# One kernel for a scan block and two MLPs: fewer jobs in the preparation stage, in a deeper pipeline, and other engines for two of its operations

## Time and profile before

| | |
|---|---|
| median of 3 runs | 3308.22 us |
| the profiled execution | 3307.34 us |
| its span (first to last instruction) | 3305.5 us |
| busy: TensorE / VectorE / ScalarE / POOL | 3123.4 / 2032.1 / 998.7 / 1085.0 us |
| granted TensorE clock, mean | 0.983 |
| matmuls of the MLP stage (L809, L825) | 750.9 + 743.6 us |
| matmuls of the gated MLP (L682, L703) | 539.3 + 523.8 + 523.3 us |

### The profile page before, as it was taken

The page is one execution under the profiler, slowest core; times in us unless marked ns, Lnnn a source line. Parts: engine busy times, 40 slices in busy tenths (PEclk is TensorE's granted clock), DMA queues, the critical chain, the costliest instruction groups (busy, mean ns, idle before and its releaser), DMA issues.

```text
span 3305.5 us, 43287 instructions
## 1 busy us (share of the span) xinstructions
PE 3123.4 (94%) x15308; PEld 2523.5 (76%) x15308; DVE 2032.1 (61%) x4502; ACT 998.7 (30%) x1719; POOL 1085.0 (33%) x1082
## 2 busy tenths in 40 slices
PE   3679999999998999999999899999999999999999
PEld 2557777777777777777777688888888888888887
DVE  8778888888886666666677654444444444444442
ACT  3235555532223333333332322122211122121211
POOL 6655555554444444444444311011111110101100
PEclk8889999999999999999999999999999999999999
DMA  3122222236654455455543422222222222222210
GB/s 100 51 69 66 90 87 73 79 95 153 153 138 101 134 147 144 127 146 141 130 117 77 116 51 52 36 51 52 51 46 52 42 51 47 47 49 44 52 20 26
DMA packets 594855, 272.65 MB, mean 82 GB/s; under 512 B 425040, under 2 KB 516432, under 8 KB 592080
## 3 DMA queue, kind: packets, MB, share of 16 engines
q1 hardware_dynamic: 594640, 269.88, 32.9%
HBM read 193.75 MB, written 76.05 MB: 82 GB/s over the span
## 4 chain that ended last, share of the span: by engine, by line
PE 61%; DVE 20%; issue 7%; POOL 7%; ACT 3%; SPq 1%; DMA 1%; DVEq 0%; ACTq 0%; POOLq 0%
PE bank L825 21%; PE bank L809 21%; PE bank L682 11%; PE bank L703 5%; DVE qs L931 3%; POOL qa L1441 3%; DVE qa L948 3%; POOL qa L1435 2%; DVE ub L1008 2%; DVE sg L903 2%; DVE qs L942 2%; DVE qb L956 2%; PE bank L745 2%; DVE qa L906 2%; DVE qs L936 1%
## 5 line engine op out<-in xcount | busy, mean ns | idle before, releaser
L809 PE MATMUL bank<-hT,Wp 128*128 128x512 f32 x3072 | 750.9, 393 | 2.5 <-ACT gf L1388 2.5
L825 PE MATMUL bank<-Wp,G 128*128 128x512 f32 x3072 | 743.6, 391 | 0.0
L825 PEld LDWEIGHTS bank<-Wp,G 128*128 128x128 f32 x3072 | 576.5, 188 | 125.9 <-DVE G L1161 0.4
L809 PEld LDWEIGHTS bank<-hT,Wp 128*128 128x128 f32 x3072 | 573.3, 188 | 124.1 <-ACT gf L1388 3.0
L682 PE MATMUL bank<-XT,Wg 128*128 128x512 f32 (+1 forms) x2148 | 539.3, 401 | 42.8 <-DVE XT L963 26.0
L1159 DVE CAST G<-gf 128x512 fp32r<-128x512 f32 x256 | 110.4, 431 | 754.7 <-PE bank L825 753.4
L682 PE MATMUL bank<-XT,Wu 128*128 128x512 f32 (+1 forms) x2148 | 523.8, 393 | 37.1 <-DVE sg L903 37.1
L703 PE MATMUL bank<-Wd,HT 128*128 128x512 f32 x2112 | 523.3, 397 | 2.0 <-POOL HT L1449 1.6
L682 PEld LDWEIGHTS bank<-XT,Wg 128*128 128x128 f32 x2148 | 402.8, 194 | 143.1 <-DVE XT L963 37.5
L682 PEld LDWEIGHTS bank<-XT,Wu 128*128 128x128 f32 x2148 | 405.5, 192 | 128.2 <-issue 45.4
L703 PEld LDWEIGHTS bank<-Wd,HT 128*128 128x128 f32 x2112 | 392.8, 189 | 95.3 <-issue 13.1
(11 more groups left out here) (98 smaller groups left out, 2793.1 us busy)
## 6 DMA issues: line engine op xcount, KB each, us to landing
px<-in_L_attn_x_dram SPq DMA_DIRECT2D x128, 256.0 KB, 3.0
xin<-in_L_attn_x_dram SPq DMA_DIRECT2D x128, 256.0 KB, 3.7
sT<-r_K SPq DMA_DIRECT2D x128, 256.0 KB, 4.1
r_Z<-xin SPq DMA_DIRECT2D x64, 256.0 KB, 2.1
r_U<-ub SPq DMA_DIRECT2D x16, 1024.0 KB, 6.4
sU<-r_U SPq DMA_DIRECT2D x32, 512.0 KB, 4.9
r_Y<-sY SPq DMA_DIRECT2D x16, 1024.0 KB, 5.8
xl<-in_L_attn_x_dram SPq DMA_DIRECT2D x64, 256.0 KB, 2.9
```

The source lines that it names most:

```text
L809: ins = e.matmul(bk[:], Wp[f][wh][:, 0, k * P:(k + 1) * P], hT[xh][b % 2][:, k, :], start=(k == 0 and p_ == 0), stop=(k == KD - 1 and p_ = ...
L825: ins = e.matmul(ACC[j][:], G2[gh][:, n % 2, j * P:(j + 1) * P], Wp[f][wh][:, 1, :], start=(f == 0 and p_ == 0), stop=(f == 15 and p_ == 2))
```

## The change

- The head holds 32 jobs: 28 weights and tiles 0 to 3. The other six weights and tiles 4 and 5 become side jobs of windows 1 to 8, and windows now run from 1 (`SW`), with all h jobs in them.
- The head's pipeline is deeper: roundings two jobs behind, `dequant` three, high and low four. Magnitudes alternate between two PSUM banks, transposed jobs between two others.
- In the head the low part is made in PSUM: after ScalarE has written the high part, TensorE adds it, multiplied by minus identity (`nI`), to the transposed job (`minus_high`), and ScalarE copies the rest out (`low`). In windows VectorE still makes low parts, now ahead of h's transpose.
- The small multiplication by `SHRINK` of the head's weights goes from POOL to ScalarE.
- `uwrite` goes from VectorE to ScalarE as `Identity(scale*x + bias)`, with a new small operation `offset` (`nb`) for the bias; it starts in window 66.
- Statistics: one tile a window. Taps start in window 11 and skip windows that transpose a side job. `w_high` and `w_low` run two steps ahead of use, from window 176 to step 13.

```diff
-SW = 10
-K0 = 13
-UW0 = 64
+SW = 1
+K0 = 11
+UW0 = 66
...
-ORDER = "DDWWDDXWWXXWXWDDWWWWWHDHDWHXXHWWHWWHDDWHDWHWWDWWH"
...
+HEAD = ([("w", i) for i in range(14)] + [("x", 0), ("x", 1)] + [("w", i) for i in range(14, 28)]
+        + [("x", 2), ("x", 3)])
...
+SIDE = {w - 27: ("w", w) for w in range(28, 34)}
+SIDE.update({7: ("x", 4), 8: ("x", 5), NF - 1: ("x", 6), NF: ("x", 7)})
+SIDE.update({NF * i + o: ("x", 4 * i + j) for i in range(2, NB) for o, j in ((-7, 0), (-4, 1), (-2, 2), (-1, 3))})
...
+def magnitude_bank(m):
+    if m < NJ:
+        return (4, 6)[m % 2]
+    return 4 if m < MSSM and JOBS[m][0] == "h" else None
...
+TAPS = [s for s in range(K0, S0) if s - 2 not in SIDE][0:32]
...
             if m < NJ:
-                b = bank[5] if TPOS[m] <= NTWO and TPOS[m] % 2 else bank[7]
+                b = bank[(5, 7)[TPOS[m] % 2]]
...
+            def minus_high(m):
+                nk = job_width(m) // P
+                e.wait_ge(s_hi, TPOS[m])
+                if TPOS[m] == 1:
+                    e.wait_ge(s_ni, 1)
+                e.matmul(turned(m).rearrange("p (k c) -> p k c", c=P), nI[:], job_dst(m)[0], start=False, stop=True,
+                         skip_group_check=True
+                         ).then_inc(s_ng, 1)
...
+            for m in range(NJ):
                 turn(m)
+                minus_high(m)
+                if 18 <= m < 26:
+                    gu_half(0, (m - 18) // 4, range((m - 18) % 4, (m - 18) % 4 + 1))
...
                 h_mult(s - 1)
                 if low_x is not None:
                     low(low_x)
+                h_rows(s - 1)
                 front(h)
...
-            for m in range(NJ + 3):
+            for m in range(NJ + 2):
                 if m < NJ:
...
                     biggest(m)
...
+                if m >= 2:
+                    mid_a(m - 2)
                 if m < NJ:
                     inverse(m)
...
+                if m >= 2:
+                    mid_b(m - 2)
...
+            def weight_inverse(m):
+                if HEAD[m][0] == "w":
+                    r_ = qs[:, m % 4, 1, 0:job_width(m) // 16]
+                    e.wait_ge(s_rc, m + 1)
+                    e.activation(r_, r_, ACT.Copy, scale=SHRINK).then_inc(s_rw, 1)
+
+            def low(m):
+                e.wait_ge(s_ng, TPOS[m])
+                e.activation(job_dst(m)[1], turned(m).rearrange("p (k c) -> p k c", c=P), ACT.Copy).then_inc(s_lo, 1)
...
+            def uwrite(t):
...
+                e.wait_ge(s_nb, rooted(t))
...
+                for i in range(2):
+                    ins = e.activation(
+                        ub[:, :, j, 8 * i:8 * i + 8].rearrange("p (s j) k -> p s j k", j=2),
+                        px[:, n % 4].rearrange("p (s i j k) -> p i s j k", i=2, j=2, k=8)[:, i],
+                        ACT.Identity, bias=nb[:, t:t + 1], scale=rst[:, b, 1, j:j + 1])
+                ins.then_inc(s_uw, 1)
...
+            for m in range(NJ + 4):
+                if m >= 4:
+                    high(m - 4)
+                if m < NJ:
+                    weight_inverse(m)
                 if 1 <= m <= NJ:
                     magnitude(m - 1)
+                if m >= 4:
+                    low(m - 4)
...
-                if 0 <= s - (NW - 7) < 8:
-                    w_high(s - (NW - 7))
+                if 0 <= s - (NW - 3) < 4:
+                    w_high(s - (NW - 3))
...
-                if 8 <= n + 6 < 16:
-                    w_high(n + 6)
+                if n + 2 < 16:
+                    w_high(n + 2)
...
+            for m in range(NJ + 3):
+                if m < NJ:
+                    scale(m)
+                if m >= 3:
+                    dequant(m - 3)
                 if m < NJ:
                     scaled(m)
```

More of the change, by code:

```diff
@@ L55, in pairs @@
     return sorted((n for n in range(NP) if first(n) <= w <= last(n)), key=lambda n: n % 3)
-ORDER = "DDWWDDXWWXXWXWDDWWWWWHDHDWHXXHWWHWWHDDWHDWHWWDWWH"
[L61 to L69, removed]
-NJ = len(HEAD)
[L72 to L75, removed]
+HEAD = ([("w", i) for i in range(14)] + [("x", 0), ("x", 1)] + [("w", i) for i in range(14, 28)]
+        + [("x", 2), ("x", 3)])
+NJ = len(HEAD)
+SIDE = {w - 27: ("w", w) for w in range(28, 34)}
+SIDE.update({7: ("x", 4), 8: ("x", 5), NF - 1: ("x", 6), NF: ("x", 7)})
+SIDE.update({NF * i + o: ("x", 4 * i + j) for i in range(2, NB) for o, j in ((-7, 0), (-4, 1), (-2, 2), (-1, 3))})
+SIDES = [SIDE[s] for s in sorted(SIDE)]
+SWIN = {job: s for s, job in SIDE.items()}
 JOBS = list(HEAD)
@@ L90, with side @@
 NTH = sum(m < NJ for m in TURNS)
[L92 to L98, removed]
+def side(s):
+    return JOF[SIDE[s]] if s in SIDE else None
 def h_job(s):
@@ L722, in ssm_states @@
                     e.wait_ge(s_q, MSSM)
-                    e.wait_ge(s_lo, max(TPOS[x_job(w)] for w in XFRONT if w + 2 < S0 - 1))
+                    e.wait_ge(s_lo, max(TPOS[side(w)] for w in SIDE if w + 2 < S0 - 1))
                     e.wait_ge(s_kV, 16)
@@ L763, in window @@
                     gu_half(s, 1)
-                if x_job(s - 2) is not None:
-                    turn(x_job(s - 2))
+                if side(s - 2) is not None:
+                    turn(side(s - 2))
                 if 0 <= k < 2 * NV and k % 2:
@@ L1068, in window @@
                 k = s - S0
-                h, x_ = h_job(s), x_job(s)
-                fronted, low_x = x_job(s - 1), x_job(s - 3)
+                h, x_ = h_job(s), side(s)
+                fronted, low_x = side(s - 1), side(s - 3)
                 outputs = 0 <= k < 2 * NV and k % 2
@@ L1317, in window @@
                 k = s - S0
-                if x_job(s - 3) is not None:
-                    high(x_job(s - 3))
+                if side(s - 3) is not None:
+                    high(side(s - 3))
                 if s - 2 >= SW - 1:
@@ L1337, in window @@
                     ssm_inputs(k // 2 + 1)
-                if x_job(s) is not None:
-                    magnitude(x_job(s))
+                if side(s) is not None:
+                    magnitude(side(s))
                 if 0 <= k < 2 * NV and k % 2:
@@ L1481, in window @@
                 k = s - S0
-                h, x_, fronted = h_job(s), x_job(s), x_job(s - 1)
+                h, x_, fronted = h_job(s), side(s), side(s - 1)
                 if s - 2 >= SW - 1:
```

240 lines of the change are left out of this document (101 added, 139 removed).

## The result

The kernel after takes 3286.57 us, median of four runs (3284.65 to 3288.47); the kernel before, beside it, 3308.14 us. The ratio is 0.9937, with a 95% interval of 0.992 to 0.9955: faster, by 21.6 us. The forecast was 44 us faster, at 3263; the range held the time. The profiled execution took 3286.65 us with a span of 3284.9.

A forecast was written before the change was run, and what follows sets the result against it. VectorE was taken to pace the head, TensorE the MLP, with short TensorE waits between. Terms -19 - 11 - 12 + 7 - 3 - 6 = -44 took 3307.3 to 3263 us; range 3238 to 3298.

The forecast's parts named there:

- first multiplication at: End of the head, position 0: 32 jobs at 2.7 us each, POOL slowest, put its multiplication at 102.6.
- from there to position 15: Windows 1 to 15: 132.8 us priced singly, 8.4 of VectorE's waits for high parts, 3 for cold TensorE.
- windows 16 to 63: TensorE's waits on side tiles' low parts and on Silu before transposes shrink: minus 11, bounds 0 and minus 21.6.
- windows 64 to 97: Recurrence input moves from VectorE to ScalarE, ending TensorE's waits on VectorE's multiplication: minus 12, bounds 0 and minus 20.
- Silu 97 to 99: Recurrence start: later writes delay POOL's memsets, table loads and the next input tile: plus 7, bounds 0 and plus 14.
- windows 99 to 163: New order of low part and h's transpose shortens waits on low: minus 3, bounds 0 and minus 8.
- windows 164 to 178: Four MLP weights' splits move to the MLP's first steps, relieving VectorE: minus 6, bounds 0 and minus 12.
- The ring that I priced at 2.4: Head: per job, high part, minus-high, next transposes, high again, between ScalarE and TensorE, about 2.4 us with hand-overs.
- the rival of a ring at 3.4: Head: ScalarE-TensorE hand-overs, not POOL, set the pace at 3.4 us a job; 22 us come back, 3285; chance 0.15.
- the rival of windows at half clock: Windows 1 to 9: TensorE's short idle stretches hold its clock at the lower level; slower, 3316; chance 0.06.
- It doesn't do what it says: Windows 16 to 98 keep 23 us of waits under other names, head gives 10 less: 3296; chance 0.08.
- more than I count: No high-part waits, Silu waits of windows 16 to 63 gone, recurrence start unchanged: 3240, POOL perhaps gaining too; chance 0.13.

The follow-up runs named there:

- f5: Kernel after with tap rows stored earlier, e2b's taps, recurrence input written from window 64, low part in PSUM and `nI` made at the third job: 3265.55 us.
- e6: Kernel after with the head's low parts back on VectorE, without the minus-identity matmul and ScalarE's copy, pipeline still deep: 3287.3 us.
- e9: Kernel after with the head's pipeline as shallow as before, low parts still made in PSUM: 3308.41 us.
- e10: e9 with the low parts on VectorE, so a shallow head without the minus-identity matmul: 3307.06 us.
- e1: Kernel after with SP storing each group's row of taps one window after the group's last taps, not three: 3277.55 us.
- e2: e1 with the taps in two of every three windows, as before the change: 3283.29 us.
- e2b: e1 with the taps kept out of the windows just ahead of a transposing one, not out of the transposing ones: 3274.54 us.
- e8: e1 with VectorE's order in a window as before, h's transpose ahead of the side job's low part: 3275.13 us.

## Why the prediction was right or wrong

| term | forecast | measured |
|---|---|---|
| first multiplication at | 102.6 | 113.8 |
| from there to position 15 | 144.2 | 141.7 |
| so position 15, against 265.9 | -19 | -10.4 |
| windows 16 to 63 | -11 | +8.1 |
| windows 64 to 97 | -12 | -13.4 |
| Silu 97 to 99 | +7 | +7.9 |
| windows 99 to 163 | -3 | -2.8 |
| windows 164 to 178 | -6 | -8.4 |
| MLP stage | 0 | -1.6 |

The right column, from the third row on, adds up to the 20.6 us between the spans. Of the 23.4 us that the forecast had too much, windows 16 to 63 are 19.1 and the head 11.2; the other terms gave 7 back.

**The head: wrong by 11.2 us, and its premise too.** The period was right: forecast at 2.7 us with POOL as the slowest engine, and 2.56 with POOL full (from 30 to 90 us, input tiles and all, it is busy 86%, not above 90). The ring that I priced at 2.4 turns in 2.34. So the rival of a ring at 3.4 fell, and that its time, 3285, is the measured one is chance. What was missed lies around the period. The fourth job's reduce starts at 15.75, not 13.2 (+2.6): ScalarE makes `nI` first in its program and waits 6.3 us for the constants, holding the first `SHRINK` multiplication (f5 bears it out). The next five jobs take 15.1, not 14.0 (+1.1), because a root step of 128x8 elements between them takes 0.98 us. The four input tiles cost 8.3 us over the period instead of 1.6 (+6.7): VectorE's normalisation waits for TensorE's transposes of four jobs back, 7.2 us in four waits. The gate pieces put in for six jobs' time add 1.5. Against that stand 3.2 gained by the shorter period. The last job's way out takes 14.2, not 11.7 (+2.5): its rounded values are ready at 106.6, but TensorE transposes them at 108.87, after job 30's minus-high, for the ring of the jobs ahead is still turning. These add up to 11.2. VectorE's wait and ScalarE's in the head:

```profile
DVE qa L922 <- PE bank L659: 7.2, 4, 2.8
...
ACT nI L1404 <- DMA cs<-in_constants_dram: 6.3, 1, 6.3
```

The premise was that "VectorE sets the pace" of the head before, by the 3.03 us of its five operations, and that the low part's leaving frees it. The sum of lengths was no bound (e6: 2.60). While weights were prepared POOL set the pace, with four operations in 3.05 us; the earlier trace rows has three of them, and the two sums lie so near each other that the wrong engine fitted too. What gives the gain is the depth (e9, e10, against a shallow head slower than that of before) and, by POOL's rows, the move of `SHRINK`, which no run undid.

**Positions 0 to 15: right in size.** The windows priced one by one from the earlier trace rows held to 2.5 us in sum; VectorE waits 7.2 us in six windows for a weight's high part, where I took 8.4 in seven. But VectorE was not the fullest engine and not over 90% busy: it is busy 119 of 141.7 us and TensorE 126, so what paces these windows is not settled. The granted clock was 0.95: the rival of windows at half clock fell.

**Windows 16 to 63: the failed step.** "I take 10 of the 12.4 and 1 of the 9.2." The 12.4 did fall by 8, but the waits on Silu rose by as much (e1 against before: 21.9 and 21.6 in sum). I treated the two waits as independent, when where the taps stand sets both (e2, e2b): a tap moved out of one window stands in the next. That is the rival "It doesn't do what it says", for this stretch. The 9 us of window 27 were in no case of mine: I read the new tap windows, but not where SP's stores, tied to them by `+ 3`, come to stand.

**Windows 64 to 98: right**, with ScalarE's half at the top of my bounds, in windows 64 to 98:

```profile
L1305 ACT ACTIVATE ub<-px,nb,rst 128x256 f32<-128x256 f32 x124 | 64.1, 589 | 0.0
```

I had taken 0.5 from bounds of 0.3 and 0.6. It hid all the same, as ScalarE is 133 us busy of 295. The Trainium skill, ScalarE: Activation LUTs, section "What ACT_TABLE_LOAD costs", charges operands read through a pointer extra; by its formula a 256-column one with two of them would take 585 ns, an estimate. The trace agrees, with 589. The few us that the rival "more than I count" let POOL gain when the writes left VectorE did not show: POOL is busy 146.0 us in this stretch before and 147.9 after, with 127 instructions in both.

**The rest: right in size.** That the 2.8 us of windows 99 to 163 come from the new order is not shown (e8). In windows 164 to 178 the wait on the multiplication fell from 18.2 to 11.5:

```profile
PE bank L687 <- DVE sg L901: 11.5, 10, 2.9
```

**What stays open.** How much of the head's gain is the depth and how much the move of `SHRINK`. The input tiles' wait was read from the trace and not tried. The sizes of single stretches under 2 us rest on one profile each.

## What to carry to other kernels

Before you credit an engine with being the bound of a pipelined stage, look at the distance between the starts of its operations and at its idle time, not at the sum of their lengths, and do so for every engine: the one whose operations follow each other without a gap is the bound (here POOL). When a trial undoes one part of a change, ask whether the parts that stay (here `SHRINK` on ScalarE) make the undone version worse than the old one was. When work moves between windows, list everything that hangs on its window number, the stores in the in-order queue above all, and ask what each stands behind. Count two waits fed by one cause (here the exponentials' places) as one sum: the change moved them and the sum stayed, 21.6 and 21.9 us, and only one of the other places tried lowered it, to 16.6.

## What the runs showed of the hardware

- VectorE's operations overlap. In e6 operations of 0.68 us start 0.60 apart, the 0.34 reciprocal costs 0.26.
- Some VectorE operations last until POOL's operation ends. VectorE and POOL in the head of the kernel after, in order of time:

```profile
14.55 1.06 POOL L1450 TENSOR_TENSOR qa<-xin,qs 128x512 f32<-128x512 f32 x1 [0.86 <-ACT qs L1234]
14.60 1.03 DVE L873 TENSOR_SCALAR rst<-rtmp 128x8 int32<-128x8 int32 x1
15.66 0.17 DVE L877 TENSOR_TENSOR rtmp<-rst 128x8 f32<-128x8 f32 x1
...
17.93 1.06 POOL L1450 TENSOR_TENSOR qa<-xin,qs 128x512 f32<-128x512 f32 x1
...
18.03 0.98 DVE L885 SCALAR_TENSOR_TENSOR rst<-rtmp,rst 128x8 f32<-128x8 f32 x1
```

The steps on 128x8 elements (L873, L885) end at 15.63 and 19.01, POOL's operations at 15.61 and 18.99; L877, with POOL idle, takes 0.17. Long operations are held too when both inputs lie in SBUF, and are not when one lies in PSUM. The second rounding over the whole run, least, median and longest ns, with the magnitude in `qb` (SBUF) and in `bank` (PSUM):

```profile
L962 DVE SCALAR_TENSOR_TENSOR qb<-qb,qa x150: 424/693/1649, 122.8 to 1849.4; 128x512 f32<-128x512 f32 x143, 128x384 f32<-128x384 f32 x4, 128x256 f32<-128x256 f32 x3
L962 DVE SCALAR_TENSOR_TENSOR qb<-bank,qa x127: 424/691/694, 14.1 to 975.4; 128x512 f32<-128x512 f32 x124, 128x256 f32<-128x256 f32 x3
```

The one of 1.65 us (at 367.00) runs beside two POOL operations that take 1.26 and 1.51 us (at 366.84 and 368.06), where POOL's 128x512 operations take 1.06 in the head. The Trainium skill, GPSIMD Engine Reference, section "Specifications", names contention for the SBUF interfaces for VectorE instructions with two SBUF inputs or in a two-port mode; the trace agrees for L885 and L962 (two inputs in SBUF), and it shows the price, up to 1.0 us an operation. No run took the POOL operation away.

- A matmul of 512 columns alone, with minus identity, takes 0.79 us by its row in a stretch where the granted clock is 1.00, and ScalarE's copy that waits for it starts 0.83 us after its start (105.94 and 106.77); in the dense MLP stage one takes 0.225 on average.
